# Ranking two of four token chunks inside the last self-attention steps, gathering on 32-column tiles, and ranking the other two inside the first feed-forward half

## The reference

```python
x = x + attn(_layernorm(x), wq, wk, wv, wo)            # self-attention
h = _layernorm(x)
scores = jnp.einsum('bsd,d->bs', h, w_router)          # one per token
top_scores, top_idx = jax.lax.top_k(scores, k)         # k = 32 of the 64 tokens of a batch
selected = jnp.take_along_axis(h, top_idx[:, :, None], axis=1)
g = jax.nn.gelu(jnp.einsum('bkd,df->bkf', selected, W1) + b1)   # f = 2048
processed = jnp.einsum('bkf,fd->bkd', g, W2) + b2
x = x + h.at[top_idx].add(jax.nn.sigmoid(top_scores)[:, :, None] * processed)
```

## Time and profile before

| what | value |
|---|---|
| median of 3 runs | 1358.81 us (1358.48 to 1359.64) |
| profiled execution, its own time | 1359.8 us |
| its span, first to last instruction | 1358.0 us |
| PE busy | 1335.4 us, 98% of the span |
| last self-attention step written out (1127.10 to 1156.49) | 29.39 us |
| first four feed-forward tiles (1156.49 to 1196.03) | 39.54 us |

### The profile page before, as it was taken

The page is one execution under the profiler, slowest core; times in us unless marked ns, Lnnn a source line. Parts: engine busy times, 40 slices in busy tenths (PEclk is TensorE's granted clock), DMA queues, the critical chain, the costliest instruction groups (busy, mean ns, idle before and its releaser), DMA issues.

```text
span 1358.0 us, 33086 instructions
## 1 busy us (share of the span) xinstructions
PE 1335.4 (98%) x12984; PEld 1055.4 (78%) x12984; DVE 670.5 (49%) x1686; ACT 732.6 (54%) x1414; POOL 543.9 (40%) x284
## 2 busy tenths in 40 slices
PE   7999999999999999999999999999999999999998
PEld 6877777777777777777777777777888887878786
DVE  4254544544445445444444545547566668732323
ACT  5456656656566566656656656664333457453231
POOL 6552422432332242243233235635434344566342
PEclk9999999999999999999999999999999999999999
DMA  7011010110111111111101113010000002222241
GB/s 257 26 59 34 27 58 25 33 58 25 33 37 46 33 33 50 33 33 50 33 33 50 33 33 118 14 56 1 2 0 0 0 2 78 80 86 100 78 140 62
DMA packets 39332, 66.19 MB, mean 49 GB/s; under 512 B 4208, under 2 KB 8560, under 8 KB 39280
## 3 DMA queue, kind: packets, MB, share of 16 engines
q1 hardware_dynamic: 38848, 64.67, 14.5%
q10 hardware_dynamic: 432, 0.79, 0.2%
HBM read 61.25 MB, written 4.19 MB: 48 GB/s over the span
## 4 chain that ended last, share of the span: by engine, by line
PE 89%; DVE 2%; ACT 2%; POOL 1%; issue 1%; POOLq 0%; DVEq 0%; ACTq 0%
PE psum L204 39%; PE psum L961 9%; PE psum L252 8%; PE psum L1844 6%; PE psum L1813 5%; PE psum L222 5%; PE psum L240 5%; PE psum L261 3%; PE psum L976 3%; PE psum L1493 1%; PE psum L986 1%; PE psum L994 1%; PE psum L1004 1%; PE psum L1824 0%; PE psum L1032 0%
## 5 line engine op out<-in xcount | busy, mean ns | idle before, releaser
L302 ACT ACTIVATE PT<-psum 128x512 f32<-128x512 f32 x256 | 153.2, 598 | 226.5 <-PE psum L252 226.5
L289 ACT ACTIVATE prob<-prob,nmx 128x512 f32<-128x512 f32 x256 | 182.6, 714 | 94.4 <-DVE nmx L344 94.4
L358 DVE COPY V<-psum 128x512 f32<-128x512 f32 x128 | 88.6, 692 | 229.7 <-PE psum L204 229.7
L344 DVE CUSTOM_DVE_ANT_0 prob<-psum,mbias 128x512 f32<-128x512 f32 x256 | 165.5, 684 | 67.0 <-PE psum L222 67.0
L295 ACT ACTIVATE prob<-prob,rinv 128x512 f32<-128x512 f32 x256 | 182.6, 713 | 0.0
L491 POOL TENSOR_SCALAR ctx_a<-ctx_r 128x1536 fp32r<-128x1536 f32 x16 | 65.4, 4088 | 265.4 <-PE psum L204 265.2
L491 POOL TENSOR_SCALAR ctx_b<-ctx_r 128x1536 fp32r<-128x1536 f32 x16 | 65.4, 4088 | 252.7 <-PE psum L204 235.6
L252 PEld LDWEIGHTS psum<-ident,prob 128*128 128x128 f32 x1024 | 127.4, 141 | 34.8 <-issue 1.3
L252 PE MATMUL psum<-ident,prob 128*128 128x128 f32 x1024 | 153.2, 272 | 0.6 <-ACT PT L302 0.4
L204 PE MATMUL psum<-wv_h,ctx_b 128*128 128x512 f32 x384 | 144.4, 417 | 0.0
L204 PE MATMUL psum<-wv_h,ctx_a 128*128 128x512 f32 x384 | 142.2, 412 | 1.2 <-DVE K L358 1.2
(11 more groups left out here) (217 smaller groups left out, 2811.6 us busy)
## 6 DMA issues: line engine op xcount, KB each, us to landing
ctx_r<-in_ctx SPq DMA_DIRECT2D x32, 768.0 KB, 4.6
w_r<-in_L_ffn_W SPq DMA_DIRECT2D x64, 256.0 KB, 2.8
xres<-in_x SPq DMA_DIRECT2D x16, 256.0 KB, 2.7
out<-tok SPq DMA_DIRECT2D x13, 256.0 KB, 3.5
tok<-in_x SPq DMA_DIRECT2D x3, 1024.0 KB, 12.0
mask<-in_mask_BxS_bf SPq DMA_DIRECT2D x32, 64.0 KB, 4.1
tok<-in_x SPq DMA_DIRECT2D x4, 256.0 KB, 3.7
wq_r<-in_L_xattn_Wq SPq DMA_DIRECT2D x4, 256.0 KB, 5.5
```

What stands on the lines that cost most here:

```text
L289: act.activation(prob[:, r, :], prob[:, r, :], ACT.Exp, bias=nmx[:, r:r + 1], scale=-1.0, accum_out=rsum[:, r:r + 1]).then_inc(s_ex, 1)
L302: act.activation(PT[:, r, :, :].rearrange("p k n -> p (k n)"), T_bank, ACT.Copy).then_inc(s_Pt, 1)
L344: dve.tensor_tensor_reduce(prob[:, r, :], S_bank[r], mbias[:, b, :], 1.0, 3.0e38, ALU.add, ALU.min, nmx[:, r:r + 1]).then_inc(s_mx, 1)
L358: dve.tensor_copy(item_place(q, m), KV_bank[m % 2]).then_inc(s_KVe, 1)
```

## The change

**In self-attention.** The square roots for the norms of chunks 0 and 1 move from step 13 to 12. The normalizing and scoring of chunk 0 move one step earlier (ACT in steps 12 and 13, DVE in 13); its spread, comparisons and one-hots are done in step 14; chunk 1 is normalized in step 14, before that in the end. In `pe_end` the gathers of chunks 0 and 1 are put between the probabilities, values and output projections of the last two tiles. The high and low half of weight tile 0 are made in step 14 (its DMA is issued earlier, at the last `s3_XT`), tile 1 and 2 in the end.

**The gather** is cut. Before, a half took 8 products, each of 128 x 128 weights (columns of `xn4`) with 128 columns of one-hots, two of them added into the same result. Now the weights are 128 x 32 blocks at four column positions, each with only the 64 one-hot columns that can be set for that tile, and nothing is added: 32 products for a half, 64 for a chunk.

**In the feed-forward block.** Chunk 2 is ranked at n = 0 and 1 and gathered at n = 2 and 3 as before, with the transposes one tile later; chunk 3 moves from n = 1 to 3 to n = 12 to 15, as do the router weights' sigmoid. The root for chunk 3's norms moves behind the first GELU, with explicit loads of the GELU table.

**On POOL** the sums of tiles 0 to 7 leave the places behind each `split_low` and are made in pairs, at n = 2, 3, 14 and 15, behind a wait for `s5_gl`. The sums of tiles 8 to 15 are made in the loop, n = 4 to 11.

Some buffers move: `q_T` and `pT` to the room below the output weights, `dots`, `dg` and `s_all` elsewhere, other banks for the results. The diff, cut to what the steps speak of:

```diff
@@ pe3
+            if isinstance(t, int) and t == G - 2:
+                pe.wait_ge(s3_ms, G - 2)
+                pe_spread(pe, 0)
@@ dve3
+                if isinstance(t, int) and t == G - 2:
+                    dve.wait_ge(s4_on, 1)
+                    dve_compare(dve, 0, range(CH))
+                    dve_one_hot(dve, 0, range(CH))
@@ pool3
+                if isinstance(t, int) and t == G - 2:
+                    pool.wait_ge(s4_oh, CH)
+                    split_low(pool, 0, 0)
@@ ranking and gather
+        def dve_rank(dve, c):
+            for h in range(2):
+                dve_compare(dve, c, (2 * h, 2 * h + 1))
+                dve_one_hot(dve, c, (2 * h, 2 * h + 1))
@@ pe_gather
             for k in range(DT):
                 for e in range(2):
-                    ins = pe.matmul(bank4(c, 1 + h)[:, k * P:(k + 1) * P],
-                                    xn4[:, SLOT_OF[c], 2 * h + e, k * P:(k + 1) * P], oh[:, c % 2, 2 * h + e, :],
-                                    start=(e == 0), stop=(e == 1))
+                    mine = slice(e * BPG * KEEP, (e + 1) * BPG * KEEP)
+                    for r in range(4):
+                        ins = pe.matmul(bank4(c, 1 + h)[head_rows(r), k * P + mine.start:k * P + mine.stop],
+                                        xn4[:, SLOT_OF[c], 2 * h + e, k * P + r * HD:k * P + (r + 1) * HD],
+                                        oh[:, c % 2, 2 * h + e, mine], start=True, stop=True,
+                                        tile_position=(0, r * HD))
@@ dve_end
-            dve_o(dve, LAST - 1, 1 - PAR)
             dve.wait_ge(s3_ex, G)
             dve.tensor_reduce(rc3[:, 0, :], last, AX_X, ALU.add).then_inc(s3_sm, 1)
             dve.wait_ge(s3_sm, G)
             dve.wait_ge(s3_pn, LAST)
             dve.reciprocal(rc3[:, 1, :], rc3[:, 0, :]).then_inc(s3_rc, 1)
+            dve_o(dve, LAST - 1, 1 - PAR)
+            dve_rank(dve, 1)
@@ POOL, feed-forward
+                sums = {2: (0, 1), 3: (2, 3), 14: (4, 5), 15: (6, 7)}
                 def split(f, n, e, q):
                     if isinstance(n, int) and n == 0:
+                        return
+                    if isinstance(n, int) and n == 1:
                         pool.wait_ge(s4_oh, 2 * CH)
-                    if isinstance(n, int) and n == 1:
+                    if isinstance(n, int) and n == 2:
                         pool.wait_ge(s3_PV, G)
                     split_low(pool, n, e)
-                    if isinstance(n, int) and n == 1:
-                        add(0)
-                    if q == 0 and not (isinstance(n, int) and n == 0):
-                        add(n)
+                    if q == 0 and not isinstance(n, int):
+                        pool.wait_ge(s5_gl, n - 1)
+                        add(n + CH, n)
+                    if isinstance(n, int) and n in sums:
+                        pool.wait_ge(s5_gl, n + 1)
+                        for t in sums[n]:
+                            add(t, CH * SLOT_OF[t // CH] + t % CH)
@@ DVE, feed-forward
-                between = {0: lambda: dve_scores(dve, 2),
-                           1: lambda: (dve_compare(dve, 2), dve_one_hot(dve, 2), dve_scores(dve, 3)),
-                           2: lambda: (dve_low(dve, 2, 0), dve_low(dve, 2, 1), dve_compare(dve, 3), dve_one_hot(dve, 3)),
-                           3: lambda: (dve_low(dve, 3, 0), dve_low(dve, 3, 1))}
+                between = {0: lambda: (dve_scores(dve, 2), dve_deviations(dve, REST, 2)),
+                           1: lambda: dve_rank(dve, 2),
+                           3: lambda: (dve_low(dve, 2, 0), dve_low(dve, 2, 1)),
+                           FF - 4: lambda: dve_scores(dve, 3),
+                           FF - 3: lambda: dve_rank(dve, 3),
+                           FF - 1: lambda: (dve_low(dve, 3, 0), dve_low(dve, 3, 1))}
@@ ACT, feed-forward
-                between = {0: rest, 2: lambda: (act_high(act, 2, 0), act_high(act, 2, 1), act_one_hots(act, 2)),
-                           3: lambda: (weights(), act_high(act, 3, 0), act_high(act, 3, 1), act_one_hots(act, 3))}
+                between = {0: deviations, 1: rest,
+                           3: lambda: (act_high(act, 2, 0), act_high(act, 2, 1), act_one_hots(act, 2)),
+                           FF - 3: weights,
+                           FF - 1: lambda: (act_high(act, 3, 0), act_high(act, 3, 1), act_one_hots(act, 3))}
@@ PE, feed-forward
-                           2: lambda: (pe_gather(pe, 2, 0), pe_gather(pe, 2, 1), pe_transpose(pe, 2)),
-                           3: lambda: (pe_gather(pe, 3, 0), pe_gather(pe, 3, 1), pe_transpose(pe, 3))}
+                           2: lambda: (pe_gather(pe, 2, 0), pe_gather(pe, 2, 1)),
+                           3: lambda: pe_transpose(pe, 2),
+                           FF - 2: lambda: (pe_gather(pe, 3, 0), pe_gather(pe, 3, 1)),
+                           FF - 1: lambda: pe_transpose(pe, 3)}
```

More of the change, by code:

```diff
@@ L695, in _ @@
                 act.wait_ge(s_eps, 1)
-                act.activation(warm[:], epsb[:], ACT.Sqrt, bias=epsb[:])
+                act.activation(warm, epsb[:], ACT.Sqrt, bias=epsb[:])
                 deviation(0, 2, slice(0, 2))
@@ L842, in tile @@
                         act.activation(rs3[:, 0:G - 2], mv3[:, 0:G - 2, 1], ACT.Sqrt, bias=epsb[:]).then_inc(s3_sd, 1)
-                        act.activation(warm[:], epsb[:], ACT.Exp)
+                        act.activation(warm, epsb[:], ACT.Exp)
                     if last and q == 1:
@@ L1122, in act3 @@
                     copy(p_place(h), bank[h]).then_inc(s3_pa, 1)
-            if isinstance(t, int) and t >= G - 3:
-                act_deviations(act, FIRST if t == G - 3 else MIDDLE)
-                act.activation(warm[:], epsb[:], ACT.Exp)
+            if isinstance(t, int) and t == G - 4:
+                act_deviations(act, FIRST)
+                act.activation(warm, epsb[:], ACT.Exp)
+            if isinstance(t, int) and t == G - 2:
+                act.wait_ge(s3_K, G)
+                act_normalize(act, 1, (0, 1))
             if has(t - 1):
@@ L1291, in perceiver_layer @@
         KB = 1024
-        SLOT_OF = (3, 1, 2, 0)
+        SLOT_OF = (3, 0, 1, 2)
         XN = len(SLOT_OF)
@@ L1576, in act_end @@
             copy(high, src).then_inc(s3_oa, 1)
-            for f in range(3):
-                act_split(act, f)
-            act.wait_ge(s4_nm, 2)
-            act_normalize(act, 2, range(2))
+            act_high(act, 0, 0)
+            act_high(act, 0, 1)
+            act_deviations(act, MIDDLE)
+            split_high(act, 1, 1)
+            act_one_hots(act, 0)
             for h in range(2):
@@ L1656, in _ @@
                 sp.dma_start(b2_sb[:], b2.rearrange("(a n) -> a n", a=1).broadcast_to([P, D])).then_inc(s4_c, 16)
+                sp.wait_ge(s3_XT, G)
+                load(sp, 0, 0, 0)
                 sp.wait_ge(s3_V, G)
-                for f in range(DEEP):
+                for f in range(1, DEEP):
                     load(sp, f, f, f)
@@ L1759, in _, with deviations, rest @@
                 act_end(act)
+                def deviations():
+                    act_deviations(act, REST)
+                    act.activation(warms[:, 1:2], epsb[:], ACT.Gelu_apprx_tanh)
+                def rest():
+                    act.wait_ge(s4_nm, 3)
+                    act_normalize(act, 3)
                 def weights():
```

151 lines of the change are left out of this document (75 added, 76 removed).

## The result

The changed kernel takes 1371.26 us, the median of 6 runs from 1369.65 to 1372.64; the kernel before, run beside it, 1359.56 (1358.48 to 1359.96, 6 runs). The ratio is 1.0087, 95% interval 1.0074 to 1.0100: slower by 11.7 us, under 1% but clear of the noise. The forecast was 1362.5, its range ended at 1366.0, so the sign was right and the size was not.

What follows compares the result with a forecast made beforehand. It took PE, busy 98% of the span, as the bound: -6.0 (gather) - 6.5 (waits) + 0.5 (new waits) + 13.3 (stalls) + 2.4 (clock) = +3.7 us, giving 1362.5 us, range 1358.8 to 1366.0.

Steps and rivals of the forecast that it cites:

- all three stalls: Feed-forward block: PE waits for POOL's low halves at H(3), H(4) and H(15), 6.5, 2.3 and 4.5 us, sum 13.3.
- The gather half: Each chunk's gather: a half on small tiles takes 1.03 us, so four chunks save 6.0 us.
- the stall's price isn't given back later: After the feed-forward stalls: nothing that follows has slack to give their 13.3 us back.
- the waits in the last step: Last self-attention step: all four PE waits get cover, part of 6.5 us saved together with the feed-forward waits.
- The new wait of the last projection: Last self-attention step: 0.4 us waiting for DVE's low half and a little more before the last projection, 0.5 in all.
- "What is removed", (1) and (2): Gather, and waits in the last self-attention step and first feed-forward tiles: savings of 6.0 and 6.5 us.
- the signs at the prediction's end: Listed trace checks; for the last self-attention step, no idle over 0.6 us and an end about 6.2 us earlier.
- 4.5 is nearer to 1.50, so it stays: PE's clock at H(15): after 4.5 us idle it narrowly stays up, so no extra time there.
- The fall of the clock: At H(3), after 6.5 us idle, PE's clock falls and H(3) takes 5.1 instead of 2.72: 2.4 us more.
- the clock falls in the third stall too: Rival at H(15): clock falls there too, or stays low longer; 2.4 to 4 us more, 1365 to 1366.5, chance 0.20.
- the third stall: Feed-forward, n = 14: PE waits 4.5 us between H(14) and H(15) for POOL's low half.
- The second stall: Feed-forward, between H(3) and H(4): PE waits 2.3 us for POOL's low half.

Runs made afterwards that it cites:

- e4: The changed kernel with the gather of before (8 matmuls of 128 x 128 a half): 1368.27 us, ratio 1.0065 to the kernel before.
- e9: e1 with the old gather for the second half of chunks 0 and 1 only: 1351.53 us, ratio 0.9944 to the kernel before.
- e1: The changed kernel with POOL's paired sums waiting for the gelu output two tiles earlier: 1357.77 us, ratio 0.9983 to the kernel before.
- e2: The changed kernel with feed-forward weight tiles from 2 on fetched after the last self-attention values: 1368.32 us, ratio 1.0061 to the kernel before.
- e10: e3 with each matmul of chunk 2's gather issued three times, writing the same values: 1360.10 us, one run.
- e3: The changed kernel with the edits of both e1 and e2: 1353.90 us, ratio 0.9957 to the kernel before.
- e7: e1 with the wait for the newest tile's gelu output kept at tile 3 alone: 1358.89 us, ratio 0.9997 to the kernel before.
- e8: e1 with the wait for the newest tile's gelu output kept at tile 14 alone: 1362.62 us, ratio 1.0019 to the kernel before.

## Why the prediction was wrong

**Right.** The mechanism and place of all three stalls: 6.36, 2.00 and 4.24 us against 6.5, 2.3 and 4.5, together 12.6 against 13.3 (bounds 12 and 15), released by the row named in advance. The gather half (1.03). That the stall's price isn't given back later (the tail, 101.90 twice). That the waits in the last step can be covered: e4 and e9 show PE busy throughout it. The new wait of the last projection, taken as 0.5, is not there in e9.

**The step that failed first: "What is removed", (1) and (2), in the last self-attention step.** It took a gather half at 1.03 from a stretch where 64 such matmuls stand among slower ones, and used that as its price anywhere. In the last step two halves and the values between them are some 190 small matmuls in a row, and PE ran out of instructions, once in each chunk. Against the 6.6 us that the step was to gain by the sum (the signs at the prediction's end say 6.2) stand gaps of 3.28 + 1.68 = 4.96 us and slow products worth 6.20 - 4.59 = 1.6, in sum 6.6; the step came out 0.1 shorter. e9 takes the instructions away and gains 6.5 against e1 in this stretch. No rival of mine had this, so the range was too low by it: without these 6.5 us the changed kernel would have taken 1364.8, inside the range. It could have been suspected: the page of before has an instruction queue with transfers, and an "issue" row is a question, not an answer.

**The step that failed second: "4.5 is nearer to 1.50, so it stays".** The fall of the clock was the right mechanism, one time out of three. It fell behind all three stalls, the shortest 2.00 us: 2.78 + 1.89 + 2.49 = 7.2 us against my 2.4. Less 0.7, by which the stalls were shorter, that is 4.1 over the forecast; the stretch shows 3.4 (13.7 measured, and 13.3 + 2.4 - 3.0 for two gathers - 2.4 for waits = 10.3 forecast), and 0.7 isn't assigned. The rival "the clock falls in the third stall too" had about this size, with a chance of 0.20. I drew a threshold half-way between 1.50 and 7.92 us from two rows; nothing in the trace stood for it, and it would have been better to take the fall as likely behind each stall. What fails in every run is the third stall: the clock falls behind its 4.24 or 4.25 us in all five traces that have it. The second stall's 1.89 was partly chance, since in e2 the clock stays up behind 2.15 us at the same place.

**In sum.** 6.5 (last step) + 3.4 (H(0) to H(16)) = 9.9, less the 0.8 by which the last step began earlier, is 9.1. With the forecast's +3.7 that makes +12.8, and the spans differ by 12.8.

**Open.** What asks for the next block of instructions, and so how early it could be had, no run here shows. The gaps under the same burst range from 2.55 to 3.28 us as their transfers come 2.2 to 2.7 us after the block began; why a transfer comes that late, and not at another time, isn't shown. The Trainium skill (DMA: Bandwidth & Descriptors, Queues, rings and completion order) says that a transfer engine takes turns between its queues packet by packet; that would make an instruction transfer late in a burst, and the direction agrees, but the wait of a single packet isn't in these profiles.

## What to carry to other kernels

A piece of POOL or DVE work is free only as long as nothing urgent is queued behind it: before a wait is put ahead of it, follow that queue to the next thing PE needs. Cutting a matmul into small tiles saves array time and spends instructions: count how many PE instructions in a row the new code issues, and how long PE is busy with each 256 of them; here, with quiet transfers, the next 256 could be used 2.8 and 3.55 us after the last began, and later under a burst. And price a stall of 2 us or more with the slow products behind it: those of more than 4 us read here cost another 1.8 to 2.8 us each, and of three of about 2 us two cost 1.8 and 1.9, the third 0.35.

## What the hardware showed that I had not expected

- PE's instructions arrive in blocks that hold 128 matmuls with their loads, and with idle transfers the next block was usable 3.55 us after the last began in e10, and about 2.8 in e3 (2.0 for its 128 records and the gap of 0.85). 128 small matmuls need 1.99. In the first place the gap is 0.85 to 1.42 us without the burst of weights, and 2.55 to 3.28 with it.
- The length of an idle time alone doesn't say whether the clock falls. It fell behind 2.00 (changed kernel) and 2.15 us (e7); it stayed behind 2.15 (e2, at the same product), 2.46 (e10, the next 128 in 1.99) and 2.55 (e7, the next 38 in 0.76). Behind 3.07 us in e8 the next 38 still took 0.76, and only what came after them was slow. The column of the granted clock showed 0.94 and 0.92 for the two stretches here, where at the kernel's start it had read 1.00 beside slow products.
- A DVE dot product of 0.68 us takes 1.78 or 2.86 beside POOL's operations.
